# 16x8-head attention layers: two buffers each for the parts of q and k, and other steps at 256 keys

## The reference

```
x = x + L0_attn(norm(x))            x = x + L0_xattn(norm(x), ctx)      x = x + L0_ffn(norm(x))
x = x + L1_attn(norm(x), Wk, Wq, Wo, bo)      # the layer whose order changes
...
x = x + L3_xattn(norm(x), ctx)      x = x + L3_ffn(norm(x))
```

```
scale = e ** (-0.25)                                   # e = 128
k = (x @ Wk).reshape(b, t, h, s).transpose(0, 2, 1, 3) # h = 16, s = 8
q = (x @ Wq).reshape(b, t, h, s).transpose(0, 2, 1, 3)
v = (x @ Wk).reshape(b, t, h, s).transpose(0, 2, 1, 3)
dot = einsum('bhqd,bhkd->bhqk', q * scale, k * scale)
out = einsum('bhqk,bhkd->bhqd', softmax(dot), v)       # then @ Wo + bo
```

## Time and profile before

| | us |
|---|---|
| median of 3 runs | 2432.0 |
| lowest, highest run | 2421.03, 2434.09 |
| profiled execution: its time | 2436.32 |
| profiled execution: span | 2434.6 |
| PE busy | 2024.1 (83%) |
| DVE busy | 1483.5 (61%) |
| ACT busy | 1117.5 (46%) |
| POOL busy | 592.0 (24%) |
| mean granted PE clock | 0.885 |

### The profile page before, as it was taken

How to read it: one execution, slowest core, us unless ns; L and a number is a source line. 1 busy time by engine, 2 the same in 40 slices (tenths; PEclk the granted TensorE clock), 3 DMA queues, 4 the chain that set the end, 5 groups by cost and what they waited for, 6 DMA issues and landing times. The chain is left out here.

```text
span 2434.6 us, 37694 instructions
## 1 busy us (share of the span) xinstructions
PE 2024.1 (83%) x12579; PEld 1210.1 (50%) x12579; DVE 1483.5 (61%) x3501; ACT 1117.5 (46%) x2834; POOL 592.0 (24%) x799
## 2 busy tenths in 40 slices
...
GB/s 33 28 97 64 83 41 41 91 200 144 146 59 92 68 54 33 10 0 36 1 1 1 1 1 32 1 31 3 39 1 2 1 1 1 76 81 88 86 50 27
DMA packets 128494, 112.56 MB, mean 46 GB/s; under 512 B 62215, under 2 KB 101168, under 8 KB 126000
## 3 DMA queue, kind: packets, MB, share of 16 engines
...
## 5 line engine op out<-in xcount | busy, mean ns | idle before, releaser
L957 DVE TENSOR_REDUCE L_xattn_mx<-L_xattn_psS 128x1 f32<-128x512 f32 x512 | 326.2, 682 | 116.0 <-PE L_xattn_psS L1082 111.8
L1192 ACT ACTIVATE L_xattn_PT<-L_xattn_psT 128x512 f32<-128x512 f32 x512 | 283.0, 600 | 95.5 <-PE L_xattn_psT L1094 90.0
L603 ACT ACTIVATE L_attn_pr<-L_attn_psS,L_attn_negm 128x256 f32<-128x256 f32 (+1 forms) x512 | 221.9, 446 | 103.5 <-DVE L_attn_negm L403 67.4
L1082 PE MATMUL L_xattn_psS<-L_xattn_KR,L_xattn_QR 72*128 72x512 bf16 x512 | 213.0, 421 | 44.2 <-DVE L_xattn_mx L957 21.1
L401 DVE TENSOR_REDUCE L_attn_mx<-L_attn_psS 128x2 f32<-128x512 f32 x256 | 164.9, 686 | 114.8 <-PE L_attn_psS L512 114.7
L1094 PE MATMUL L_xattn_psT<-L_xattn_QR,L_xattn_KR 75*128 75x256 bf16 x1024 | 198.4, 279 | 3.7 <-ACT L_xattn_PT L1192 1.8
L1108 PE MATMUL L_xattn_psO<-L_xattn_PT,L_xattn_V 128*32 128x256 f32 x2048 | 192.5, 398 | 3.2 <-ACT L_xattn_PT L1192 1.1
L2068 DVE TENSOR_TENSOR L_ffn_act<-L_ffn_act,L_ffn_cwb 128x512 f32<-128x512 f32 x128 | 86.7, 690 | 130.2 <-ACT L_ffn_act L2198 106.1
L512 PE MATMUL L_attn_psS<-L_attn_qk 64*128 64x256 f32 x1024 | 146.4, 404 | 11.7 <-ACT L_attn_pr L603 11.7
L2133 PE MATMUL L_ffn_psU<-L_ffn_hT,L_ffn_wup 128*128 128x512 f32 x256 | 133.5, 612 | 13.9 <-ACT L_ffn_act L2198 13.9
L2198 ACT ACTIVATE L_ffn_act<-L_ffn_psU 128x512 f32<-128x512 f32 (+1 forms) x132 | 78.5, 597 | 135.6 <-PE L_ffn_psU L2133 131.8
...
## 6 DMA issues: line engine op xcount, KB each, us to landing
...
```

The source lines that it names most:

```text
L603: ins = nc.scalar.activation(pr[n % 3][:, r, t, 0:width], psS[(2 * n + r) % 3][:, t, 0:width], ACT.Exp, bias=negm[:, n % 4, t, r:r + 1], s ...
L957: nc.vector.reduce_max(mx[:, b % 2, u, hd:hd + 1], psS[n % 2][:], AX.X).then_inc(s_used, 1)
L1082: ins = nc.tensor.matmul(psS[n % 2][:, i * keys:(i + 1) * keys], QR[b % NB][0:PAIR, hd, t * P:(t + 1) * P], KR[b % NB][0:PAIR, hd, :], sta ...
L1192: nc.scalar.activation(PT[n % NPT][:, 2 * u:2 * u + 2], psT[i % NPS][:], ACT.Exp).then_inc(exp_ready, 1)
```

## The change

In all three layers qs and ks become two buffers each, used in turn by even and odd batches, with a semaphore for each. ACT and the splitting engine then wait for the copies of batch b - 2 instead of b - 1. With 256 keys (L1_attn alone) the table of steps changes as well:

| | before | after |
|---|---|---|
| Q, K, V after T (b > 0), steps | 2, 4, 6 | 4, 6, 8 |
| steps from T(b) to T(b+1) in the ramp (APART) | 7 | 9 |
| T of batches 1, 2, 3, 4, 5 | -17, -10, -3, 12, 28 | -17, -8, 1, 12, 28 |
| Q of batches 1, 2, 3, 4, 5 | -15, -8, -1, 14, 30 | -13, -4, 5, 16, 32 |
| K of batches 1, 2, 3, 4, 5 | -13, -6, 1, 16, 32 | -11, -2, 7, 18, 34 |
| V of batches 1, 2, 3, 4, 5 | -11, -4, 3, 18, 34 | -9, 0, 9, 20, 36 |
| stage and spread of batches 1, 2, 3, 4, 5 | -9, -2, 6, 24, 40 | -10, -1, 8, 24, 40 |
| M of (0,0), (0,1), (1,0), (1,1), (2,0) and rows | -9, -1, 7, 15, 23 | the same |
| A and O of batch b | 16b+24, 16b+25 | 16b+25, 16b+26 |

```diff
@@ -656,11 +656,11 @@
-    LEAD, PREP, STAGE, EARLY, DVE_SPLITS = (HH + 6, 38, 7, 3, 2) if from_ctx else (HH + 10, 52, 9, 6, 3)
+    LEAD, PREP, STAGE, EARLY, DVE_SPLITS = (HH + 6, 38, 7, 3, 2) if from_ctx else (HH + 10, 52, 9, 4, 3)
...
-    APART, BACK = (4, 6) if from_ctx else (7, 8)
+    APART, BACK = (4, 6) if from_ctx else (9, 9)
...
-    FIRST, LAST = -LEAD, NH + (16 if head_major else 10)
+    FIRST, LAST = -LEAD, NH + (16 if head_major else BACK + 2)
@@ -671,9 +671,9 @@
-        for i, kind in ((0, "K"), (2, "T"), (3, "Q")) if from_ctx else ((0, "T"), (2, "Q"), (4, "K")):
+        for i, kind in ((0, "K"), (2, "T"), (3, "Q")) if from_ctx else ((0, "T"), (4, "Q"), (6, "K")):
...
-        jobs[max(H * b - LATE_V, FIRST) if from_ctx else at + 6 * (b > 0)].append(("V", b, 0))
+        jobs[max(H * b - LATE_V, FIRST) if from_ctx else at + 8 * (b > 0)].append(("V", b, 0))
@@ -704,7 +704,7 @@
-        qs, ks = sb("qs", [P, PARTS, S], BF16), sb("ks", [P, PARTS, keys], BF16)
+        qs, ks = ([sb(f"{n}{i}", [P, PARTS, w], BF16) for i in range(2)] for n, w in (("qs", S), ("ks", keys)))
@@ -722,15 +722,16 @@
+        q_staged, k_staged = ([sem(f"{v}_staged{i}") for i in range(2)] for v in "qk")
...
@@ -774,7 +775,7 @@
-                        sp.dma_start(q_dram[b % 2, i].rearrange("d h c -> h d c"), qs[:, i]).then_inc(q_staged, 16)
+                        sp.dma_start(q_dram[b % 2, i].rearrange("d h c -> h d c"), qs[b % 2][:, i]).then_inc(q_staged[b % 2], 16)
@@ -782,7 +783,7 @@
-                        sp.dma_start(k_dram[b % 2, :, i].rearrange("d h c -> h d c"), ks[:, i]).then_inc(k_staged, 16)
+                        sp.dma_start(k_dram[b % 2, :, i].rearrange("d h c -> h d c"), ks[b % 2][:, i]).then_inc(k_staged[b % 2], 16)
@@ -796,12 +797,12 @@
-                    sp.wait_ge(q_staged, 16 * PARTS * (b + 1))
+                    sp.wait_ge(q_staged[b % 2], 16 * PARTS * (b // 2 + 1))
...
-                    sp.wait_ge(k_staged, 16 * PARTS * (b + 1))
+                    sp.wait_ge(k_staged[b % 2], 16 * PARTS * (b // 2 + 1))
@@ -853,13 +854,13 @@
-            wait(eng, q_staged, 16 * PARTS * b)
-            split(eng, link, qf, qs, q_split)
+            wait(eng, q_staged[b % 2], 16 * PARTS * (b // 2))
+            split(eng, link, qf, qs[b % 2], q_split)
...
-            wait(eng, k_staged, 16 * PARTS * b)
-            split(eng, link, kf, ks, k_split)
+            wait(eng, k_staged[b % 2], 16 * PARTS * (b // 2))
+            split(eng, link, kf, ks[b % 2], k_split)
@@ -1156,11 +1157,11 @@
-                        (qf, qs, S, q_staged, q_split, q_high, bq_s, scale) if kind == "Q" else (kf, ks, keys, k_staged, k_split, k_high, bk_s, 1.0))
+                        (qf, qs[b % 2], S, q_staged[b % 2], q_split, q_high, bq_s, scale) if kind == "Q" else (kf, ks[b % 2], keys, k_staged[b % 2], k_split, k_high, bk_s, 1.0))
...
-                    wait(act, staged, 16 * PARTS * b)
+                    wait(act, staged, 16 * PARTS * (b // 2))
```

4 lines of the change are left out of this document (2 added, 2 removed).

## The result

The changed kernel takes 2411.38 us (median of 7 runs, 2400.92 to 2415.62). The kernel before takes 2423.62 (7 runs, 2418.34 to 2434.09; the three that stand ahead of the prediction are among them, and two of those three lay high). The ratio is 0.9942, 95% interval 0.9924 to 0.9959, so 0.58% or 14.1 us faster. The plain difference of the medians is 12.2 us. The forecast, 2418.0 against 2432.0, is a ratio of 0.9942 too. That all four digits agree is luck: the interval goes from 10 to 18 us. The changed kernel run again beside the last experiment gave 0.9931, 0.9906 to 0.9955.

A forecast was written before the change was run, and what follows sets the result against it. The prediction held that no engine is full and that stops in which PE, VectorE and ACT all stand bound L1_attn. 9.4 us by step 23 plus 4.6 after made 14.0, so 2418.0 us against 2432.0; range 2410 to 2430.

The forecast's parts named there:

- the forecast's own case: Whole program: 14.0 us gained, 2418.0 us against 2432.0, own range 2413.5 to 2422.5; chance 0.43.
- (a): L1_attn's loop: landing of the spread's bytes sets when rows arrive, so term B is 0 to 1; 2422.1 us; chance 0.20.
- (b): Ramp's gain given back at steps 12 and 16, 4 us, and term B lost; 5.4 us gained, 2426.6; chance 0.16.
- (c): L1_attn's long stretch: stops shrink below what costs the clock, 5 us on top; 19 us gained, 2413; chance 0.13.
- term B: L1_attn, steps 23 to 87: 4.6 us gained as maxima splits go ahead of q on POOL, some clock included.
- Part 1: Two buffers for qs and ks: worth 0 in the 512-key layers, between 0 and 1 us either way.
- (e): L1_attn's ramp: the moved stage alone frees Q(2) of its wait, buffers idle; alters no number, given no chance.
- Part 2: L1_attn's ramp: ACT's stops of 8.4 us removed, step 0 begins 8.8 us earlier, bounds 6 and 10.
- Part 3: L1_attn, steps 0 to 23: stop of about 2 us at M(1,1); 9.4 us gained by step 23, bounds 5 and 11.
- the thin cover: Step 12 of L1_attn: T(4), at about 781.8, needs norm(4), done by about 780; cover of 2 us.
- Part 4: L1_attn, steps 23 to 87: a loop of maxima, rows and spreads closes over each period; gain 4.6 us, term B.
- (d): Loop also covers steps 7 to 23: stops of some 4 us at M(1,1) to M(4,0); 3.8 us slower, 2435.8; chance 0.08.

The follow-up runs named there:

- e3: Changed kernel with new steps of Q, K, V only for batches 0 to 3, later batches and A, O as before: 2418.15 us, 0.9973 of the kernel before.
- e1: Both buffers of qs and ks, table of steps as in the kernel before: 2420.72 us, ratio 0.9993 to the kernel before.
- e2: New table of steps with single buffers of qs and ks, edited from the kernel before: 2406.55 us, ratio 0.9934 to it.
- e4: Changed kernel with POOL splitting the maxima ahead of any other job of the same step: 2410.19 us, ratio 0.9938 to the kernel before.
- e8: Changed kernel with e4's edit and the second head half of each spread sent 8 steps later: 2397.29 us, ratio 0.988 to the kernel before.
- e5: Changed kernel with A and O of each batch one step earlier, as before the change: 2413.0 us, ratio 0.9952 to the kernel before.

## Why the prediction was right and where it was wrong

**The mechanism and the size held.** Step 0 came 9.1 us earlier for 8.8. The change took 10.6 us to M(2,0) for 9.4, and 4.5 us more to M(6,0) for 4.6 (3.8 in the mean of all executions). The ratio 0.9942 is that of the forecast, in its last digits by luck. The time itself, 2411.4, is 6.6 us under the forecast, mostly because the kernel before has its median at 2423.6 and not at 2432.0.

**The step that failed is the weighing of the cases, and the bound in it above all.** The prediction took 0.5%, 12.2 us, as the least that can be told from no change, had 14.0 as its own sum, and yet gave "within" 0.48 and "faster" 0.47, so that no clear change was its likeliest outcome. It got there by letting a third of the forecast's own case and nearly all of (a) and (b), 0.36 together, lie under the bound. The runs showed two things in its place. First, a much smaller change can be told: the change is faster by 0.58%, 0.41 to 0.76, so the interval is 4.2 us to either side, and e3's 6.5 us still stands clear of none (0.9956 to 0.9989). With a bound of that size the forecast, (a) with its 9.9 us, (b) with its 5.4 (just) and (c) all count as faster, 0.92 together. The prediction had no row for the 0.5%, only three runs of one kernel. Second, neither (a) nor (b) came as priced: term B was 3.8 to 4.5 us and not 0 to 1, and the 4 us that (b) gave back at steps 12 and 16 have no row.

**Part 1, the buffers.** Right in the 512-key layers (e1: 0.9993). In L1_attn the text credited them together with the moved stage and left the question to (e). e1 and e2 answer it: the new steps do it all, without the buffers.

**Part 2, the ramp.** Right, through stage(1) ahead of the rows. The rows (0,0) were just in time, as forecast. ACT's wait there was for PE, 1.56 us.

**Part 3, steps 0 to 23.** The row of five pieces on POOL was there and made the split of (1,0) 3.4 us late. The stop at M(1,1) was 0.64 us and not 2. The stop moved to M(2,0) with 3.82 us, for the rows (1,1) that stand behind a spread, where the prediction had ACT's natural time and the landing 0.6 to 1.3 us apart. M(2,0) itself was only 1.2 us off. T at step 12 did not wait for norm(4): the thin cover held.

**Part 4 and rival (a).** The rule and the two rows that the prediction set against its own term were right about the floor: rows are usable about 10 us after the spread's first issue, however early they are issued. They were wrong as a price of the change. In three of the four periods of the kernel before the rows went out 7.6 to 9.2 us behind the spread, so late that ACT's read stood 1.1 to 2.9 us above a floor of 10. The change brought all of them to between 10.1 and 11.3, not below. That is 3.5 of the 4.5 us in this pair of executions, and the second execution of the changed kernel divides its gain otherwise. The reason that the prediction gave, the late maxima split on POOL, fits the rows, and e3 shows that term B comes with the steps of Q, K and V. That POOL's order alone makes it is not shown. A still earlier split adds nothing (e4). The 1.0 us in the pieces from M to the spread I can't attribute.

**The other rivals.** (b): norm(4) and the rows of (1,0) cost nothing at step 16. (c): the granted clock stayed 0.89 in the long stretch, so the change brought no clock back that can be told. From M(2,0) to M(6,0) it was 0.93 before and 0.94 after, but 0.89 in the second execution after, so the part of term B that the prediction laid to the clock is not shown. e8 shows that the clock does come back there once the stops are gone, 4.3 us of PE's time. (d): M(2,0) did get a stop of 3.8 us, as (d) had it, but M(3,0) none and M(4,0) 0.86. The stops add up to what they were before, not to 16. (e) is shown, but for which of the new steps does it.

**The tail.** The prediction had no gain behind step 87 and allowed a loss of 1 us. From M(6,0) to the last output projection the profile shows a gain of 2.0 us, 42.35 after 44.3. Of these, 0.9 to 1.1 come behind M(7,1) and belong to the later A and O (e5), which the prediction had counted as a cost. The rest lies between M(6,0) and M(7,1), where one kernel's executions differ by as much (24.99 and 23.87 for the change), and stays open.
